# The attention mask written by ScalarE into the scores' bank, and the router's product one turn earlier

## What is computed

```
def _L0_attn_ref(x, w_qkv, ...):
    ...
    dots = jnp.einsum('bhid,bhjd->bhij', q, k) * jnp.exp(temperature)
    eye = jnp.eye(n, dtype=bool)
    dots = jnp.where(eye, NEG_MAX, dots)
    attn = jax.nn.softmax(dots, axis=-1)
    out = jnp.einsum('bhij,bhjd->bhid', attn, v)
    ...
def _L0_ffn_ref(x, gate_w, w1, w2, w3, sw1, sw2):
    logits = xf @ gate_w.T
    wts, idx = jax.lax.top_k(logits, K)
    wts = jax.nn.softmax(wts, axis=-1)
    ...
    y = y + jax.nn.gelu(xf @ sw1.T, approximate=False) @ sw2.T
h = _L0_tok_ref(x, L0_tok_W, L0_tok_b)
h = h + _L0_attn_ref(_layernorm(h, axis=-1), ...)
h = h + _L0_ffn_ref(_layernorm(h, axis=-1), ...)
```

## Time and profile before

| | us |
|---|---|
| median of 3 runs | 681.94 |
| lowest and highest run | 681.7, 683.13 |
| span of the profiled execution | 680.9 |
| TensorE busy in it | 644.8 |
| VectorE | 412.1 |
| GpSimd | 321.5 |
| ScalarE | 287.2 |

### The profile page before, as it was taken

How to read it: one execution, slowest core, us unless ns; L and a number is a source line. 1 busy time by engine, 2 the same in 40 slices (tenths; PEclk the granted TensorE clock), 3 DMA queues, 4 the chain that set the end, 5 groups by cost and what they waited for, 6 DMA issues and landing times.

```text
span 680.9 us, 14415 instructions
## 1 busy us (share of the span) xinstructions
PE 644.8 (95%) x4269; PEld 540.1 (79%) x4270; DVE 412.1 (61%) x1064; ACT 287.2 (42%) x655; POOL 321.5 (47%) x336
## 2 busy tenths in 40 slices
PE   5999999999999999999999999999779989999993
PEld 4677888778887888877888787778568979999993
DVE  7876666666666666666666667775445233555550
ACT  4334445444454444544445444344453433334431
POOL 2455445454454544545445454447834004555553
PEclk8989999999999999999999999999898998999997
DMA  8611334343543333433324332112245222333330
GB/s 303 262 52 34 81 81 120 78 102 84 111 116 82 98 88 77 115 86 93 93 77 109 92 89 55 35 36 67 76 113 205 73 59 40 40 45 47 43 48 5
DMA packets 70133, 59.70 MB, mean 88 GB/s; under 512 B 6752, under 2 KB 58848, under 8 KB 69728
## 3 DMA queue, kind: packets, MB, share of 16 engines
q1 hardware_dynamic: 63472, 55.21, 30.4%
q0 software_dynamic: 6640, 4.22, 4.5%
HBM read 16.78 MB, written 26.30 MB: 63 GB/s over the span
## 4 chain that ended last, share of the span: by engine, by line
PE 83%; DVE 6%; POOL 5%; issue 3%; ACT 1%; DMA 1%; SPq 0%; ACTq 0%; DVEq 0%; POOLq 0%
PE bank L1209 75%; POOL sorted_rows L481 2%; PE bank L1265 2%; PE bank L1418 2%; PE bank L1388 1%; POOL z L466 1%; PE bank L1509 1%; PE bank L1324 1%; POOL rstd L475 1%; PE bank L1315 0%; PE bank L1270 0%; POOL z L468 0%; PE bank L1269 0%; DVE utl L770 0%; DVE z L876 0%
## 5 line engine op out<-in xcount | busy, mean ns | idle before, releaser
L1209 PE MATMUL bank<-whigh,uth 128*128 128x512 f32 x512 | 168.9, 410 | 1.2 <-DVE lowt L770 1.2
L1209 PEld LDWEIGHTS bank<-whigh,uth 128*128 128x128 f32 x512 | 92.4, 190 | 28.0 <-issue 7.4
L1209 PE MATMUL bank<-whigh,utl 128*128 128x512 f32 x256 | 101.6, 397 | 0.0
L554 POOL DMA_INDIRECT out<-prob,ids x39 | 60.9, 1561 | 83.5 <-ACT prob L731 81.7
L475 POOL TENSOR_TENSOR rstd<-rstd,powers 128x1 f32<-128x1 f32 x64 | 35.2, 551 | 120.2 <-DVE rstd L863 64.6
L466 POOL TENSOR_TENSOR z<-z 128x512 f32<-128x512 f32 x32 | 42.3, 1321 | 91.0 <-DVE z L876 91.0
L1209 PE MATMUL bank<-xvo,x 128*128 128x128 f32 x624 | 77.6, 278 | 0.4 <-issue 0.4
L1209 PEld LDWEIGHTS bank<-xvo,x 128*128 128x128 f32 x624 | 74.1, 195 | 0.7 <-issue 0.7
L1209 PE MATMUL bank<-xT,qkw 128*128 128x128 f32 x512 | 63.6, 278 | 0.0
L1209 PEld LDWEIGHTS bank<-xT,qkw 128*128 128x128 f32 x512 | 61.0, 195 | 0.1
L1180 DVE TENSOR_TENSOR z<-tail,bank 128x512 f32<-128x512 f32 x39 | 26.8, 688 | 53.6 <-PE bank L1209 53.6
(11 more groups left out here) (223 smaller groups left out, 1332.9 us busy)
## 6 DMA issues: line engine op xcount, KB each, us to landing
sorted_rows<-blank SPq DMA_DIRECT2D x24, 709.5 KB, 5.5
xvp<-xvo SPq DMA_DIRECT2D x128, 128.0 KB
w<-w_t SPq DMA_DIRECT2D x1, 4096.0 KB, 12.1
xvo<-sorted_rows SPq DMA_DIRECT2D x39, 64.5 KB, 1.8
w<-w_high SPq DMA_DIRECT2D x4, 512.0 KB, 7.0
x_columns<-x2t SPq DMA_DIRECT2D x32, 64.0 KB
xg_in<-x_columns SPq DMA_DIRECT2D x8, 256.0 KB
levels<-w_t SPq DMA_DIRECT2D x1, 2048.0 KB, 7.5
```

The source lines that it names most:

```text
L554: nc.gpsimd.indirect_dma_start(out=out[:, :], out_offset=bass.IndirectOffsetOnAxis(ap=ids[:, j:j + 1], axis=0), in_=y[:, 2 if j == SORTED ...
L1209: return T.matmul(out_, lhsT, rhs, start=start, stop=stop)
```

## The change

ScalarE gets an instruction `set_mask`: after its exponential of turn i it copies the bf16 mask into bank 4, for the scores of turn i+1. TensorE's mask product stays in turn 0 alone; in the others the scores accumulate onto what ScalarE wrote, and wait for the semaphore `mask_set`. So bank 4 holds nothing but scores: the transposed x2 goes to bank 7, columns 128 to 255, and the logits to bank 7, columns 256 to 263. The router's product of tile i-1 now stands at the end of turn i, behind `features`, where tile i-2's stood in the middle of the turn's start. The logits' copy moves from the start of VectorE's turn to the end of ScalarE's, and TensorE waits for it ahead of the products into bank 7. In turn 31 the transpose x2_columns(30) also waits for `h2_done` of tile 31.

```
             def x2_transposed(t, first=False):
...
-                A.copy(x2t[:], B[4][:, 0:P]).then_inc(x2T_sb, 1)
+                A.copy(x2t[:], B[7][:, P:2 * P]).then_inc(x2T_sb, 1)
+
+            def keep_logits(t):
+                a.wait_ge(lg_psum, t + 1)
+                A.copy(logits[:, bass.ds(t, 1), :].rearrange("p o e -> p (o e)"),
+                       B[7][:, 2 * P:2 * P + EXPERTS]).then_inc(lg_sb, 1)
+
+            def set_mask():
+
+                A.copy(B[4][:], mask[:]).then_inc(mask_set, 1)
...
                 A.activation(prob[:], prob[:], ACT.Exp).then_inc(exp_done, 1)
+                if not is_tile(i, LAST):
+                    set_mask()
...
                 if is_tile(i, LAST):
                     gelus(1, 1, range(2))
+                if prev:
+                    keep_logits(i - 1)
+                if is_tile(i, LAST):
                     a.wait_ge(up_psum, HC)
                     x_group_hi(2, 0)
...
             a.wait_ge(att_psum, TILES)
-            gelus(1, 1, range(2, HC))
+            gelus(1, 1, range(2, 3))
+            keep_logits(TILES - 1)
+            gelus(1, 1, range(3, HC))
...
-            def keep_logits(t):
-                d.wait_ge(lg_psum, t + 1)
-                V.tensor_copy(one(logits[:, bass.ds(t, 1), :]), B[4][:, P:P + EXPERTS]).then_inc(lg_sb, 1)
...
-                if prev and older:
-                    keep_logits(i - 2)
                 if is_tile(i, LAST_BUT_ONE):
...
             finish()
-            keep_logits(TILES - 2)
-            keep_logits(TILES - 1)
...
             def x2_columns(t):
                 pe.wait_ge(x2_ready, t + 1)
-                T.transpose(B[4][:, 0:P], x2n[:], ident).then_inc(x2T_psum, 1)
+                T.transpose(B[7][:, P:2 * P], x2n[:], ident).then_inc(x2T_psum, 1)
 
             def router(t):
                 pe.wait_ge(x2T_sb, t + 1)
-                mm(B[4][:, P:P + EXPERTS], x2t[:], gateT[:]).then_inc(lg_psum, 1)
+                mm(B[7][:, 2 * P:2 * P + EXPERTS], x2t[:], gateT[:]).then_inc(lg_psum, 1)
...
-                if prev and older:
-                    router(i - 2)
                 pe.wait_ge(xT_lo, i + 1)
                 if prev and older:
-                    pe.wait_ge(h2_done, i - 1)
+                    pe.wait_ge(lg_sb, i - 1)
...
                 pe.wait_ge(g_sb, 2 * i + 2)
-                if prev and older:
-                    pe.wait_ge(lg_sb, i - 1)
-
-                T.matmul(B[4][:], ident_b[:], mask[:], start=True, stop=False)
+                if prev:
+                    pe.wait_ge(mask_set, i)
+                else:
+                    T.matmul(B[4][:], ident_b[:], mask[:], start=True, stop=True)
                 for s in range(2):
-                    last = mm(B[4][col(s, LEN), :], xT[:, col(s, LEN)],
-                              xqk[:, s, :, :].rearrange("p h k -> p (h k)"), False, True)
+                    last = T.matmul(B[4][col(s, LEN), :], xT[:, col(s, LEN)],
+                                    xqk[:, s, :, :].rearrange("p h k -> p (h k)"), start=False, stop=True,
+                                    skip_group_check=True)
...
+                if is_tile(i, LAST):
+                    pe.wait_ge(h2_done, TILES)
                 if prev:
                     x2_columns(i - 1)
                 if is_tile(i, LAST):
                     down(0, 0, range(1, GROUP), True)
-                    router(TILES - 2)
                 if f:
                     features(i + 3)
+                if prev:
+                    router(i - 1)
```

More of the change, by code:

```diff
@@ L297, in build @@
         g_psum, g_sb, vo_psum, vo_sb = sem("xqk_psum"), sem("xqk_sb"), sem("xvo_psum"), sem("xvo_sb")
+        mask_set = sem("mask_set")
         s_psum, soft, shifted, exp_done = sem("scores_psum"), sem("row_max"), sem("shifted"), sem("exp_done")
```

## The result

The changed kernel takes 685.32 us (median of 5 runs, 684.82 to 686.03), the kernel before, run beside it, 682.19 us (681.7 to 683.94): a ratio of 1.0037, 95% interval 1.0024 to 1.0051. It is slower, by 0.4%. The forecast was 684.5 us, or 2.6 us more than the kernel before; the medians of this set lie 3.1 us apart, the profiled spans 2.1. A second set of runs gave 1.0032 (1.0013 to 1.0052). The profiled executions have spans of 683.0 and 680.9 us.

A forecast was written before the change was run, and what follows sets the result against it. TensorE was taken to bound the loop, with other engines setting the pace near the end. Terms -6.0 + 11.6 - 3.8 + 0.2 + 0.6 = +2.6 on 681.9 gave 684.5 us, the forecast's own range 682 to 688.

The forecast's parts named there:

- The mask product: TensorE, turns 1 to 28: dropping the bf16 mask product gains 0.21 us a turn, -6.0 us (-8.7 at most).
- The router's stall: TensorE's loop end: branch path exposed behind the router's weight load waiting for x2t, 0.46 us a turn, +11.6 us.
- The Trainium skill's rule: TensorE's loop end: instructions wait in a queue while the sequencer goes on, which would leave only 0.04 us a turn.
- Rival A: Loop end: the sequencer runs ahead of the waiting load, router term 1.1 us, total 674.0 us; chance 0.15.
- The logits' stalls: Turns 26 to 28: TensorE's wait for VectorE's logits copy goes once ScalarE does the copy, -3.8 us.
- Rival C: Turns 26 to 28: the stall turns into one for probabilities or x columns, +3.8, 688.3 us; chance 0.15.
- The stage that GpSimd sets: From turn 28's additions on: earlier changes carry in whole; TensorE's losses inside are hidden up to 1.25 us.
- The end: After turn 30: router's wait for ScalarE's copy +0.2; turn 31: new wait and later x2 copy +0.6 us.
- The new wait: Turn 31: waiting for h2_done puts TensorE's x2 transpose 0.5 us later.
- Rival B: Loop end: half the path is hidden, 0.35 us a turn, 681.9 us, no change; chance 0.15.
- Rival D: Last turn: TensorE's half-clock stretch may come or go, +2.7 or -2.7 us on any case; no separate chance.

The follow-up runs named there:

- e1_router_next: The changed kernel with the router's product issued in the middle of the next turn's qkw products, not at the turn's end; ratio 0.9843 to the kernel before.
- e4_x2_early: The changed kernel with the x2 transpose issued before the last projection products instead of behind them; ratio 0.9876 to the kernel before.
- e7_unroll: The changed kernel with two turns in the body of TensorE's loop, 12 taken branches instead of 24; ratio 0.9934 to the kernel before.

## Why the prediction was right, and where it was not

The time, 684.5 us forecast and 685.3 measured, came out by the named mechanism, but with two errors of size that cancelled.

- **The mask product, -6.0: right.** The step to the scores is shorter by 0.21 us, and e1_router_next and e4_x2_early, without any stall, show 14.25 - 14.03 = 0.22 us a turn. ScalarE's copy took 0.58 us and nothing waited for it.
- **The router's stall, +11.6: right in its mechanism, too large in size.** That the sequencer stops at the waiting weight load was read from one row; e4_x2_early and e7_unroll show it. The failing term is the size: 14.39 - 14.03 = 0.36 us instead of 0.46 a turn, and 0.02 instead of 0.2 where no branch is taken (14.05 us behind i = 1). With the distance behind i = 1 and the three of the routing work, which are together 0.4 us longer than in e1_router_next, that is 23 x 0.36 + 0.4 = 8.7 instead of 11.6. The 0.36 us lie outside the 0.40 to 0.55 that the forecast gave to this term. The path was put right (0.62 us measured, 0.64 forecast). Wrong was what I added: 0.07 us for a second weight load, which no row of the trace showed, and the whole event path for turns without a branch.
- **The Trainium skill's rule.** The Trainium skill ("Advanced Engine Details and Errata", Sequencer and Instruction Queues) has an engine's instructions pushed into a queue, where they wait for their semaphores. My reading of it, that the sequencer goes on meanwhile, did not hold here: the branch ran 0.14 us behind the end of the copy in both kernels above, 316.8 and 311.8. Rival A fell with it.
- **The logits' stalls, -3.8: right.** The three distances shrank by 3.9 us; with the mask's share (-0.6) and the router's (+0.4) taken out, 3.7 are left. Rival C did not occur.
- **The stage that GpSimd sets: right,** nothing lost there came through (13.69 and 14.36 us, before 13.78 and 14.31).
- **The end, +0.8: wrong in size.** It is 2.9 and 3.2 us. Three steps were off. For tile 29 to 30 I took the router's wait to lie beside ScalarE's gelus; but the qkw products come 0.66 us later, and by my reading, which no run isolates, ScalarE's and VectorE's next steps with them: +0.6 instead of +0.2. The new wait, put at 0.5 us, costs 0.3. And ScalarE's copy of x2 came not 2.3 but up to 3.3 us later, because the cast of the group's columns stands behind the logits too and because the logits' copy was late; of that I had let GpSimd's scatters hide most. In the changed kernel GpSimd then sat idle for 1.3 and 2.7 us.
- **Rival B,** half the path hidden, gave 14.38 us a turn, nearly the measured distance, and forecast no change; the end made the difference. Two errors, of 2.7 and 2.1 to 2.4 us, cancelled. That the total came so near was luck, and says little for the terms.
- **Rival D,** the clock: half-clock stretches were there in every profile, 3.4 or 6.8 us long behind TensorE's wait of 2.4 us, but the sign of the result does not hang on them: in the first pair of profiles both kernels have 3.4 us of it behind the transpose of tile 29 and 6.8 in the last turn, and the changed one is still 2.1 us longer.

## What to carry to other kernels

A product at a loop's end that waits for another engine held back the branch behind it in all seven profiles that have one; ask whether the register operations and the branch still have work in front of them, and if not, move the producer earlier or the consumer behind the first products of the next turn. Here either was worth 8 to 11 us of the changed kernel's span, where the mask's saving is 6. And a copy inserted in an engine's queue delays all that stands behind it: look at the last turn separately, where nothing overlaps any more, and put first what the longest chain waits for.

## What was not expected of the hardware

- A taken branch takes 207 to 215 ns by its row in nearly every turn (231 at most in the long loop), with products still queued ahead of it or none; a turn with an exposed one is 0.32 us longer than one without.
- In the unrolled turns behind the loop a copy on ScalarE started 1.6 us after the modelled end of the product that it waited for in one profile, and 0.2 us in another of the same code. The cause is open, and so is whether the product's semaphore or ScalarE was late.
- The stretch at the 1.2 GHz level behind the same wait of TensorE was 3.4 us long in five profiles and 6.8 us in eight, although the waits differ by less than 0.1 us (2.41 to 2.48). In the last turn the same code had either: 6.8 us in the first profile of the kernel before (508.5 to 515.3), 3.4 us in the second (508.9 to 512.3).
